# Graph network, four edge layers on one core: gathers held by their predecessor's descriptors instead of by writes on GpSimd, and fewer columns by TensorE

## The chip, the cores and the metric

One core of a Trainium2 chip runs the kernel. The metric is the device time of one execution in microseconds (us); lower is better. Of each kernel several executions are timed, and one more is recorded by the hardware profiler. The engines are called as in the profile: PE (TensorE), DVE (VectorE), ACT (ScalarE), POOL (GpSimd) and SP (SyncE, which issues transfers). POOLq is POOL's sequencer, the part that reads the instructions, holds waits and hands work to the engine.

## The reference

12,500 nodes have 32 features each; 400,000 edges, sorted by their destination, go from `src` to `dst`. Four layers follow one another, each with a layer norm, a ReLU, a message per edge and a sum over the edges of each node:

```
h = relu(layernorm(x));  x = x + segment_sum(h[src] * edge_attr_32, dst) / max(degree, 1) + h
h = relu(layernorm(x));  x = x + attention(h, h[src], dst; Wq, Wk, Wv, Wo)     # softmax over a node's edges
h = relu(layernorm(x));  x = x + segment_sum(h[src], dst) @ W
h = relu(layernorm(x));  x = x + segment_sum(tensor_product(h[src], edge_attr, W), dst)
```

What all four share is `h[src]`: 400,000 rows of 32 floats, picked by index out of a table of 12,500.

## The kernel before, in words

The edges are cut into 125 chunks of 3,200: 128 partitions by 25 columns (`J`) of 32 features. A layer is a loop of 25 turns (`TURNS`) of 5 chunks (`RING`), and `rows` has five buffers, one for each chunk of a turn. The rows `h[src]` of a chunk come to it in two ways, column by column; a column is 128 rows, one for each partition.

- **By POOL.** An indirect DMA (L492) takes 128 indices from `idx` and fetches 128 rows of `h_table` from HBM. POOL's cores write its descriptors, then the DMA engines move the rows.
- **By PE.** The table lies in SBUF too (`h_parts`). A column is a tile: 14 matmuls (L690) of a one-hot matrix with the table bring 14 candidates per edge into PSUM, and DVE picks the right one (L924 and L931, or L912 in layer 1). The one-hots are made by DVE in layer 0 (L887), stored to HBM (`hots`) and loaded again in layers 1 to 3; ACT converts them (L539, L546).

`PE_COLS[layer][chunk]` says how many of the 25 columns PE takes; POOL takes the rest. In sum over a turn that is 40, 32, 40 and 28 columns of 125 by PE in layers 0 to 3, that is 8, 6.4, 8 and 5.6 for a chunk.

POOL's program for a chunk waits until the buffer is free (`rows_used`) and the indices are there (`idx_loaded`), and then repeats for each column: a gather; a wait until the last write of `pace` has ended (`pause_ended`, L495), which together with an increment of `pause_begun` (L496) makes one record in the trace; and a write of zeros to `pace`, 128 x 288 floats (L497), which nobody reads. `pauses(l, t, r, j)` is the number of writes that have gone before, plus `START` (1), which the semaphore gets at the start.

DVE waits for a whole chunk's gathers and picked tiles before it turns the rows (L1028 in layer 0, L1163 in layer 1, L1293 in layer 2, `next_rows` in layer 3); it then frees the buffer. Up to five chunks may be ahead. What else a layer does for a chunk is DVE's scans and products, and on PE the attention's sums (L738, L745) or, in layer 3, the tensor product (`spread` L764, `couple` L773), between whose steps the next chunk's tiles stand.

Before and between the loops lie the node stages: layer norm, sums over a node's edges by 98 indirect DMAs (L509; in layer 1 also L471), and small matmuls.

Of the kernel before, what the change touches and what calls it, by code (L numbers as in the profile page):

```python
# [42 lines left out]
P = 128  # L43
# [12 lines left out]
FAR = -(2.0 ** 100)  # L56
H0 = 14

PE_COLS = ((8, 8, 8, 8, 8), (7, 7, 6, 6, 6), (8, 8, 8, 8, 8), (6, 6, 5, 5, 6))
PACE = 288  # L60
PE_MAX = max(max(c) for c in PE_COLS)
BIT_BUFS = (4, 4, 4, 4)
LOOK = (4, 4, 4, 4)
# [4 lines left out]
START = 1  # L68
# [9 lines left out]
def gnn_kernel(nc, x_in, src_c, src_pe, dst_c, dst_p, dst_blocks, pattern_c, sh_c, wq, wk, wv, wo, w2, w3,  # L78
# [10 lines left out]
    KEYS = PE_MAX * (NCH + 2)  # L89
    assert NCH % RING == 0 and KT % PT == 0 and all(sum(PE_COLS[l]) % b[l] == 0 for l in range(LAYERS) for b in (TILE_BUFS, BIT_BUFS))  # L90
    assert all(sum(PE_COLS[l]) % LOOK[l] == 0 and all(n <= m for n, m in zip(PE_COLS[l], PE_COLS[0])) for l in range(LAYERS))
    assert LOOK[0] == TILE_BUFS[0] and all(LOOK[l] == BIT_BUFS[l] for l in range(1, LAYERS))
# [18 lines left out]
    with ExitStack() as ctx:  # L111
        def sb(name, shape, dt=F32):
            return ctx.enter_context(nc.sbuf_tensor(name, shape, dt))

        def sem(name):
            return ctx.enter_context(nc.semaphore(name))

        def sems(name, n=RING):
            return [sem(f"{name}{r}") for r in range(n)]
# [10 lines left out]
        idx = sb("idx", [P, RING, J], I32)  # L130
# [33 lines left out]
        mz_parts = qh[:, 0:3 * P].rearrange("p (a m) -> p a m", m=P)  # L164
        h0_width = max(PE_COLS[1]) * P // 2
        h0_keys = [work[0:H0, k, at:at + h0_width].bitcast(I16) for k, at in ((1, 0), (2, 0), (13, CH - h0_width))]
        h0_hots = [work[:, k, at:at + h0_width].bitcast(BF16) for k, at in ((8, 0), (9, 0), (11, CH - h0_width))]
        far = work[:, 9, h0_width:h0_width + H0 * D // 2].bitcast(BF16)
        pace = sb("pace", [P, PACE])
        bit_hots.append(mz[:, CH - H1 * P // 2:CH].bitcast(BF16).rearrange("p (h n) -> p h n", n=P))  # L170
        bit_hots.append(nb[:, 0:H1 * P // 2].bitcast(BF16).rearrange("p (h n) -> p h n", n=P))
        spare = work[:, 13, 6 * PC - 3 * CH:CH]
# [63 lines left out]
        rows_gathered = [sems(f"rows_gathered{a}_") for a in range(2)]  # L236
# [25 lines left out]
        mix_in, mix_ps, mix_out = sem("mix_in"), sem("mix_ps"), sem("mix_out")  # L262
        x_ready, x_stored = sem("x_ready"), sem("x_stored")

        pause_begun, pause_ended = sem("pause_begun"), sem("pause_ended")

        block = ctx.enter_context(nc.Block())

        def use(l, t, more=0):

            return t + (l * TURNS + 1 + more)

        def gathers(l, t, r, more=0):

            each = 16 * (J - PE_COLS[l][r])
            return t * each + (each * (1 + more) + (16 * TURNS * (J - PE_COLS[l - 2][r]) if l >= 2 else 0))

# [1 line left out]

        per_turn = [sum(c) for c in PE_COLS]  # L280

        def pauses(l, t, r, j):

            before = sum(TURNS * (RING * J - per_turn[k]) for k in range(l))
            return t * (RING * J - per_turn[l]) + (before + sum(J - PE_COLS[l][k] for k in range(r)) + j + START)
# [172 lines left out]

        @block.gpsimd
        def _(pool):  # L460
            pool.sem_inc(pause_ended, START)
            for l in range(LAYERS):
                if l == 0:
                    pool.wait_ge(keep_made, 1)
                if l == 1:

                    pool.wait_ge(q_zeroed, 16 * TURNS)
                    for q in range(PIECES):
                        pool.wait_ge(q_ready, q + 1)
                        for k in range(q * PT, (q + 1) * PT):  # L470
                            nc.gpsimd.indirect_dma_start(  # L471
                                out=q_edges[:, :], out_offset=bass.IndirectOffsetOnAxis(ap=begin_row[:, k:k + 1], axis=0),
                                in_=node_rows[:, k * D:(k + 1) * D], in_offset=None).then_inc(q_scattered, 16)

                    pool.wait_ge(first_loaded, 16)
                    pool.wait_ge(q_stored, 16 * PIECES)
                    nc.gpsimd.indirect_dma_start(
                        out=first_q[:, :], out_offset=None, in_=q_table[:, :],
                        in_offset=bass.IndirectOffsetOnAxis(ap=first_idx[:, :], axis=0)).then_inc(first_gathered, 16)
                    pool.wait_ge(first_gathered, 16)  # L480
                    pool.wait_ge(q_scattered, 16 * KT)
                    pool.dma_start(q_chunks[0, 0:P:D, 0:D], first_q[:, :]).then_inc(first_stored, 16)
                for a in range(2):
                    pool.wait_ge(h_stored[a], 16 * ((PIECES * (l + 1) + 1 - a) // 2))
                pool.wait_ge(parts_ready, PIECES * (l + 1))
                with pool.Fori(0, TURNS) as t:
                    for r in range(RING):
                        pool.wait_ge(rows_used[r], use(l, t, START - 1))
                        pool.wait_ge(idx_loaded[r], use(l, t) * 16)
                        pool.sem_inc(chunk_begun, 1)  # L490
                        for j in range(J - PE_COLS[l][r]):
                            nc.gpsimd.indirect_dma_start(  # L492
                                out=rows[:, r, j * D:(j + 1) * D], out_offset=None, in_=h_table[:, :],
                                in_offset=bass.IndirectOffsetOnAxis(ap=idx[:, r, j:j + 1], axis=0)).then_inc(rows_gathered[l % 2][r], 16)
                            pool.wait_ge(pause_ended, pauses(l, t, r, j))  # L495
                            pool.sem_inc(pause_begun, 1)  # L496
                            nc.gpsimd.memset(pace[:, :], 0.0).then_inc(pause_ended, 1)  # L497
                if l == 0:
                    pool.wait_ge(block_ready, 1)
                    for k in range(KT):  # L500
                        nc.gpsimd.indirect_dma_start(  # L501
                            out=blocks[:, k, :], out_offset=None, in_=dst_blocks[:, :],
                            in_offset=bass.IndirectOffsetOnAxis(ap=end_row[:, k:k + 1], axis=0)).then_inc(block_gathered, 16)
                    pool.wait_ge(node_index_ready, 1)
                for r in range(RING):
                    pool.wait_ge(outs_stored[r], 16 * (l + 1) * TURNS + START)
                table, width = (attn, 2 * D) if l == 1 else (sums, D)
                for k in range(KT):
                    nc.gpsimd.indirect_dma_start(  # L509
                        out=node_rows[:, k * width:(k + 1) * width], out_offset=None, in_=table[:, :],  # L510
                        in_offset=bass.IndirectOffsetOnAxis(ap=end_row[:, k:k + 1], axis=0)).then_inc(node_gathered[k // PT], 16)
# [1027 lines left out]
```

## Time and profile before

| | |
|---|---|
| median of 3 runs | 16,096.28 us (16,094.55 to 16,126.25) |
| span of the profiled execution | 14,816.7 us |
| the profiled execution's own time | not given by the page |
| busy: PE, DVE, ACT, POOL | 12,890.3, 9,612.6, 3,874.6, 12,431.7 us |
| gathers by POOL (L492) | 9,000 |
| writes of `pace` (L497) | 9,000 |
| mean granted clock of PE | 0.948 |

The span reaches from the first to the last instruction in the trace. The busy time of POOL does not hold the gaps between its instructions. A gather's record ends when its descriptors are written, not when its rows have arrived. In the chain of waits "issue" is time in which an engine waited for nothing that the profile shows.

### The profile page before, as it was taken

How to read it: one execution, taken by the hardware profiler on the slowest of the kernel's cores; microseconds unless marked ns; L12 is line 12 of the kernel's file. 1: busy time of each engine (PE TensorE's matmuls, PEld its weight loads, DVE VectorE, ACT ScalarE, POOL GpSimd, SP SyncE). 2: the span in 40 equal slices, each digit the busy share in tenths (PEclk: the TensorE clock that was granted, in tenths of full speed). 3: DMA queues.
4: the chain of work that ended last, by engine and by line, in shares of the span. 5: the costliest groups of instructions: out<-in, count | busy, mean ns of one | idle time of the engine just before them, and what ended most of it. 6: DMA issues, size and time to landing. Idle time of an engine off the chain costs nothing.

```text
span 14816.7 us, 226154 instructions
## 1 busy us (share of the span) xinstructions
PE 12890.3 (87%) x57644; PEld 10677.8 (72%) x57644; DVE 9612.6 (65%) x13223; ACT 3874.6 (26%) x4265; POOL 12431.7 (84%) x18594
## 2 busy tenths in 40 slices
PE   7999999992699999999689999999769999999996
PEld 6888888881577777777578888888756666767764
DVE  7666666664577777777666666666656665666665
ACT  2222222220233333333222222222211111111111
POOL 6888888887888888888778888888888888888884
PEclk9999999995899999999889999999989999999998
DMA  5444444442344444444345555545433333333332
GB/s 174 148 148 157 157 155 151 149 151 46 101 123 122 124 124 123 122 123 124 90 119 130 129 130 128 131 127 131 110 76 87 86 90 83 90 86 87 87 86 56
DMA packets 1340717, 1727.48 MB, mean 117 GB/s; under 512 B 501932, under 2 KB 1145566, under 8 KB 1339646
## 3 DMA queue, kind: packets, MB, share of 16 engines
q10 hardware_dynamic: 705956, 1154.87, 24.6%
q1 hardware_dynamic: 327194, 407.86, 9.6%
q0 software_dynamic: 306880, 158.96, 7.6%
q14 instruction: 668, 5.47, 0.1%
q8 instruction: 19, 0.31, 0.0%
HBM read 1140.23 MB, written 580.36 MB: 116 GB/s over the span
## 4 chain that ended last, share of the span: by engine, by line
POOL 41%; issue 32%; PE 20%; DVE 5%; POOLq 1%; DMA 0%; DVEq 0%; ACT 0%; ACTq 0%; SPq 0%
POOL rows L492 22%; POOL pace L497 16%; PE psum L690 12%; PE psum L773 7%; POOL outs L509 2%; PE psum L764 2%; DVE work L1340 1%; DVE work L1315 1%; POOLq L496 1%; POOL q_edges L471 1%; POOL work L501 1%; DVE tile_rows L924 0%; DVE work L1323 0%; DVE rows L931 0%; DVE outs L1347 0%
## 5 line engine op out<-in xcount | busy, mean ns | idle before, releaser
L690 PE MATMUL psum<-h_parts,one_hot 128*128 128x448 f32 x49406 | 10813.2, 377 | 482.0 <-ACT one_hot L539 262.4
L690 PEld LDWEIGHTS psum<-h_parts,one_hot 128*128 128x128 f32 x49406 | 9428.8, 192 | 1500.6 <-ACT one_hot L539 313.0
L492 POOL DMA_INDIRECT rows<-h_table,idx x9000 | 8662.9, 963 | 1966.9 <-POOL pace L497 1537.1
L546 ACT ACTIVATE one_hot<-keys 128x896 fp32r<-128x896 bf16 x2533 | 2359.9, 950 | 6435.5 <-PE psum L690 4314.0
L497 POOL MEMSET pace<- 128x288 f32 x9000 | 3213.9, 357 | 18.1 <-issue 13.2
L924 DVE TENSOR_TENSOR tile_rows<-psum,h_mask 128x448 f32<-128x448 f32 x2722 | 1686.2, 619 | 1252.3 <-PE psum L690 991.3
L931 DVE TENSOR_REDUCE rows<-tile_rows 128x32 f32<-128x448 f32 x2722 | 1677.0, 616 | 58.9
L773 PE MATMUL psum<-work,bd_t 128*128 128x512 f32 (+1 forms) x3500 | 1359.2, 514 | 240.1 <-DVE work L1323 141.3
L1323 DVE TENSOR_TENSOR work<-psum,work 128x800 f32<-128x800 f32 x875 | 862.7, 988 | 920.9 <-PE psum L764 864.2
L773 PEld LDWEIGHTS psum<-work,bd_t 128*128 128x128 f32 x3500 | 654.9, 193 | 764.4 <-issue 443.4
L912 DVE TENSOR_REDUCE rows<-psum 128x32 f32<-128x448 f32 x807 | 503.1, 623 | 792.0 <-PE psum L690 741.7
L539 ACT ACTIVATE one_hot<-work 128x896 fp32r<-128x896 bf16 x506 | 482.0, 953 | 1493.3 <-DVE work L887 1493.3
L539 ACT ACTIVATE one_hot<-bit_hot 128x896 fp32r<-128x896 bf16 x506 | 482.6, 954 | 883.4 <-DVE bit_hot L887 880.5
L1028 DVE STREAM_TRANSPOSE psum<-rows 128x800 f32<-128x800 f32 x125 | 128.2, 1026 | 864.0 <-DMA rows<-h_table,idx 864.0
L686 PE MATMUL psum<-work 128*128 128x448 bf16 x807 | 296.3, 367 | 308.0 <-DVE work L904 223.6
L745 PE MATMUL psum<-work 128*128 128x512 f32 x1500 | 524.1, 499 | 0.0
L509 POOL DMA_INDIRECT outs<-sums,end_row x294 | 291.6, 992 | 258.3 <-DMA sums<-outs 147.0
L686 PEld LDWEIGHTS psum<-work 128*128 128x128 bf16 x807 | 78.2, 97 | 501.6 <-DVE work L904 276.3
L745 PEld LDWEIGHTS psum<-work 128*128 128x128 f32 x1500 | 284.2, 189 | 210.3 <-issue 179.8
L764 PE MATMUL psum<-work,sel 120*128 120x512 bf16 x1750 | 427.4, 337 | 0.0
L1163 DVE STREAM_TRANSPOSE work<-rows 128x800 f32<-128x800 f32 x125 | 213.7, 1710 | 207.7 <-DMA rows<-h_table,idx 188.4
L1293 DVE STREAM_TRANSPOSE psum<-rows 128x800 f32<-128x800 f32 x125 | 128.2, 1026 | 289.7 <-DMA rows<-h_table,idx 289.7
(202 smaller groups left out, 6198.1 us busy)
## 6 DMA issues: line engine op xcount, KB each, us to landing
keys<-hots ACTq DMA_DIRECT2D x2542, 224.0 KB
keep_in<-keep_flat SPq DMA_DIRECT2D x2000, 100.0 KB
sums<-outs ACTq DMA_DIRECT2D x375, 400.0 KB
rows<-h_table,idx POOLq DMA_INDIRECT x9000
hots<-bit_hot ACTq DMA_DIRECT2D x506, 224.0 KB
hots<-work ACTq DMA_DIRECT2D x506, 224.0 KB
attn<-outs ACTq DMA_DIRECT2D x125, 800.0 KB
edge_in<-pattern_c SPq DMA_DIRECT2D x125, 400.0 KB
```

Of the source, the lines that this page charges most:

```text
L492: nc.gpsimd.indirect_dma_start(out=rows[:, r, j * D:(j + 1) * D], out_offset=None, in_=h_table[:, :], in_offset=bass.IndirectOffsetOnAxis( ...
L497: nc.gpsimd.memset(pace[:, :], 0.0).then_inc(pause_ended, 1)
L509: nc.gpsimd.indirect_dma_start(out=node_rows[:, k * width:(k + 1) * width], out_offset=None, in_=table[:, :], in_offset=bass.IndirectOffse ...
L539: nc.scalar.activation(one_hots[i % LOOK[l]][:, :, :], bit_hots[i % BIT_BUFS[l]], ACT.Copy).then_inc(one_hot_cast, 1)
L546: nc.scalar.activation(one_hots[i % LOOK[l]][:, :, :], loaded_hots[i % BIT_BUFS[l]], ACT.Copy).then_inc(one_hot_cast, 1)
L690: last = nc.tensor.matmul(banks[TILE_BANKS[l][b]][:, 0:H0 * D], one_hots[hot][:, h1, :], h_parts[:, part, h1 * H0 * D:(h1 + 1) * H0 * D], ...
L745: last = nc.tensor.matmul(acc_wide[:, cols], mz_parts[:, part, :], rows_in[:, cols], start=(part == 0), stop=(part == 2))
L764: last = nc.tensor.matmul(bcast[n % 2][:, cols], sel[0:SH_ROWS, n, :], shT[r][:, cols], start=True, stop=True)
L773: last = nc.tensor.matmul(acc_wide[:, cols], bd_t[:, n, :], weighted[n % 4][:, cols], start=(n == 0), stop=(n == PRODUCTS - 1))
L924: nc.vector.tensor_tensor(tile_rows[:, :].rearrange("p (f h) -> p f h", f=D), banks[TILE_BANKS[l][b]][:, 0:H0 * D].rearrange("p (f h) -> p ...
L931: nc.vector.reduce_sum(rows[:, chunk % RING, j * D:(j + 1) * D], tile_rows[:, :].rearrange("p (f h) -> p f h", f=D), axis=AX_X).then_inc(p ...
L1323: nc.vector.tensor_tensor(weighted[n % 4], bcast[n % 2], hT, ALU.mult).then_inc(weighted_ready, 1)
```

## The change

The write of `pace` and its tile go. A new semaphore `gather_written` is given to the gather as its `engine_sem`: POOL adds 1 to it when it has written the gather's descriptors. Ahead of each gather stands a wait on `gather_written` for the number of gathers before it, again with an increment behind it. `written` is the former `pauses`. Besides, PE takes 32, 24, 32 and 20 columns of a turn in place of 40, 32, 40 and 28, and POOL the rest; loops, keys and one-hots follow `PE_COLS`.

```diff
-PE_COLS = ((8, 8, 8, 8, 8), (7, 7, 6, 6, 6), (8, 8, 8, 8, 8), (6, 6, 5, 5, 6))
-PACE = 288
+PE_COLS = ((7, 7, 6, 6, 6), (5, 5, 5, 5, 4), (7, 7, 6, 6, 6), (4, 4, 4, 4, 4))
...
-        pace = sb("pace", [P, PACE])
...
-        pause_begun, pause_ended = sem("pause_begun"), sem("pause_ended")
+        gather_begun, gather_written = sem("gather_begun"), sem("gather_written")
...
-        def pauses(l, t, r, j):
+        def written(l, t, r, j):
...
-            pool.sem_inc(pause_ended, START)
+            pool.sem_inc(gather_written, START)
...
                         for j in range(J - PE_COLS[l][r]):
+                            pool.wait_ge(gather_written, written(l, t, r, j))
+                            pool.sem_inc(gather_begun, 1)
                             nc.gpsimd.indirect_dma_start(
                                 out=rows[:, r, j * D:(j + 1) * D], out_offset=None, in_=h_table[:, :],
-                                in_offset=bass.IndirectOffsetOnAxis(ap=idx[:, r, j:j + 1], axis=0)).then_inc(rows_gathered[l % 2][r], 16)
-                            pool.wait_ge(pause_ended, pauses(l, t, r, j))
-                            pool.sem_inc(pause_begun, 1)
-                            nc.gpsimd.memset(pace[:, :], 0.0).then_inc(pause_ended, 1)
+                                in_offset=bass.IndirectOffsetOnAxis(ap=idx[:, r, j:j + 1], axis=0),
+                                engine_sem=gather_written).then_inc(rows_gathered[l % 2][r], 16)
```

POOL before, in the loop of layer 0, around the border between its second and third chunk. REGISTER_ALU works out the number that the next wait compares with; `rows_used2` and `idx_loaded2` belong to the third chunk. Semaphore instructions have no row of their own; what they wait for is printed with the next instruction.

```order
L497 MEMSET pace 128x288 [waits pause_ended]
L492 DMA rows<-h_table,idx 128x32
L495 REGISTER_ALU
L497 MEMSET pace 128x288 [waits pause_ended]
L492 DMA rows<-h_table,idx 128x32 [waits rows_used2,idx_loaded2]
L495 REGISTER_ALU
L497 MEMSET pace 128x288 [waits pause_ended]
L492 DMA rows<-h_table,idx 128x32
```

POOL now, in the loop of layer 0, around the border between its first and second chunk; the lines have moved up by two.

```order
L492 DMA rows<-h_table,idx 128x32 [waits gather_written]
L490 REGISTER_ALU
L492 DMA rows<-h_table,idx 128x32 [waits gather_written]
L490 REGISTER_ALU [waits rows_used1,idx_loaded1]
L492 DMA rows<-h_table,idx 128x32 [waits gather_written]
L490 REGISTER_ALU
L492 DMA rows<-h_table,idx 128x32 [waits gather_written]
```

The wait has moved from behind the gather, where the write had it, to the front of the gather.

PE before, at the end of layer 3's loop body, where the tensor product of a chunk (L773, L764) and the tiles of the next chunk (L690) take turns:

```order
L690 MATMUL psum<-h_parts,one_hot 128x448 [waits tile_used,one_hot_cast]
L690 MATMUL psum<-h_parts,one_hot 128x448 x13
L769 REGISTER_ALU
L773 MATMUL psum<-work,bd_t 128x512 [waits weighted_ready]
L773 MATMUL psum<-work,bd_t 128x288
L679 REGISTER_ALU
L690 MATMUL psum<-h_parts,one_hot 128x448 [waits tile_used,one_hot_cast]
L690 MATMUL psum<-h_parts,one_hot 128x448 x13
L769 REGISTER_ALU
L773 MATMUL psum<-work,bd_t 128x512 [waits weighted_ready]
L773 MATMUL psum<-work,bd_t 128x288
```

PE now, at the same place:

```order
L771 MATMUL psum<-work,bd_t 128x512 [waits weighted_ready]
L771 MATMUL psum<-work,bd_t 128x288
L762 MATMUL psum<-work,sel 128x512 [waits weighted_ready]
L762 MATMUL psum<-work,sel 128x288
L767 REGISTER_ALU
L771 MATMUL psum<-work,bd_t 128x512 [waits weighted_ready]
L771 MATMUL psum<-work,bd_t 128x288
L767 REGISTER_ALU
L771 MATMUL psum<-work,bd_t 128x512 [waits weighted_ready]
L771 MATMUL psum<-work,bd_t 128x288
```

Two of the six tiles of 14 matmuls of this chunk have gone, from behind the last steps of the tensor product; four are left.

## Rows read from the trace of the kernel before

**Rows 1.** The page: busy time and the chain that ended last.

```profile
PE 12890.3 (87%) x57644; PEld 10677.8 (72%) x57644; DVE 9612.6 (65%) x13223; ACT 3874.6 (26%) x4265; POOL 12431.7 (84%) x18594
...
POOL 41%; issue 32%; PE 20%; DVE 5%; POOLq 1%; DMA 0%; DVEq 0%; ACT 0%; ACTq 0%; SPq 0%
```

**Rows 2.** The four loops: length; busy of PE, PEld, DVE, ACT, POOL; clock; DMA.

```profile
85.00:3380.00 3295.00, 3021.77 (x14208) 2715.00 (x14205) 2271.61 (x3666) 961.64 (x1009) 2871.65 (x4248) 0.97 0.48 153
3783.00:7286.00 3503.00, 3176.48 (x13869) 2537.50 (x13870) 2463.61 (x2534) 1244.38 (x1436) 3030.21 (x4636) 0.97 0.44 122
7497.00:10697.00 3200.00, 2986.04 (x14066) 2690.39 (x14064) 2072.21 (x3386) 921.97 (x1006) 2769.04 (x4238) 0.97 0.51 130
10852.00:14556.00 3704.00, 3466.44 (x14587) 2566.43 (x14587) 2279.77 (x2689) 646.08 (x680) 3152.31 (x4837) 0.98 0.33 87
```

**Rows 3.** The page's line groups on POOL: busy, mean ns, idle before.

```profile
L492 POOL DMA_INDIRECT rows<-h_table,idx x9000 | 8662.9, 963 | 1966.9 <-POOL pace L497 1537.1
L497 POOL MEMSET pace<- 128x288 f32 x9000 | 3213.9, 357 | 18.1 <-issue 13.2
```

**Rows 4.** Timeline of POOL in layer 3: start, duration, idle before.

```profile
13200.25 0.95 POOL L492 DMA_INDIRECT rows<-h_table,idx  x1 [0.17 <-POOL pace L497]
13201.19 0.36 POOL L497 MEMSET pace<- 128x288 f32 x1
13201.72 0.95 POOL L492 DMA_INDIRECT rows<-h_table,idx  x1 [0.17 <-POOL pace L497]
...
13209.71 0.95 POOL L492 DMA_INDIRECT rows<-h_table,idx  x1 [5.22 <-issue]
```

**Rows 5.** Line groups in each loop: layer 0 (two rows), layers 1, 2, 3.

```profile
L690 PE MATMUL psum<-h_parts,one_hot 128*128 128x448 f32 x14112 | 3012.6, 375 | 262.5 <-ACT one_hot L539 262.4
L492 POOL DMA_INDIRECT rows<-h_table,idx x2120 | 2116.3, 998 | 419.9 <-POOL pace L497 360.6 <-issue 59.3
L492 POOL DMA_INDIRECT rows<-h_table,idx x2318 | 2205.0, 951 | 461.1 <-POOL pace L497 400.8 <-issue 60.2
L492 POOL DMA_INDIRECT rows<-h_table,idx x2118 | 2015.1, 951 | 420.9 <-POOL pace L497 363.4 <-issue 57.5
L492 POOL DMA_INDIRECT rows<-h_table,idx x2418 | 2299.5, 951 | 526.4 <-POOL pace L497 408.7 <-issue 117.7
```

**Rows 6.** Timeline of POOL after layer 3's loop: a gather without `pace`.

```profile
14700.93 0.94 POOL L509 DMA_INDIRECT outs<-sums,end_row  x1 [0.30 <-issue]
```

**Rows 7.** Chain of waits, a turn boundary of layer 1: start, us, what.

```profile
4193.10 0.02 POOLq L490
4193.12 0.53 issue
4193.64 0.04 POOLq L495
...
4193.86 0.95 POOL rows L492
```

**Rows 8.** Chain of waits, a turn boundary of layer 0.

```profile
870.58 0.02 POOLq L490
...
871.38 0.46 POOL rows L492
```

**Rows 9.** Chain of waits, within a turn of layer 0.

```profile
3000.75 0.37 POOL pace L497
...
3001.15 0.02 POOLq L496
```

**Rows 10.** Timeline of POOL, the last gather before the boundary of rows 7.

```profile
4189.99 0.95 POOL L492 DMA_INDIRECT rows<-h_table,idx  x1 [0.17 <-POOL pace L497]
```

**Rows 11.** Busy time between the loops of layers 0 and 1.

```profile
3380.00:3783.00 403.00, 44.29 (x153) 30.25 (x153) 120.72 (x229) 22.92 (x33) 290.24 (x303) 0.54 0.19 39
```

**Rows 12.** Chain of waits in layer 3: one tile.

```profile
13002.54 2.89 PE psum L690 x14
```

**Rows 13.** Waits in total: who waited for whom, us, times, longest.

```profile
DVE psum L1028 <- DMA rows<-h_table,idx: 864.0, 116, 10.2
```

## The prediction

> **What bounds the kernel now.** I read the page first, then the busy time of the four edge loops, then POOL's line groups, its timeline and the chain of waits, because the change is on POOL's queue.
>
> The page's busy shares [rows 1] say PE 87% and POOL 84%, which does not decide it. The chain that ended last gives POOL 41%, "issue" 32% and PE 20%; the reader should see that "issue" is larger than PE and ask whose it is. The stretches of the four loops [rows 2] last 3295, 3503, 3200 and 3704 us, in sum 13,702 of the span's 14,816.7; PE is busy 3022, 3176, 2986 and 3466 us in them, so it has 214 to 327 us to spare in each. POOL's rows [rows 3] hold 9,000 gathers and 9,000 writes of `pace`. In its timeline [rows 4] gathers start at 13200.25 and 13201.72, and so on: 0.95 us of gather, 0.36 of write, 0.17 until the next gather, 1.47 in all. 9,000 x 1.47 = 13,230 us, 97% of the loops' 13,702. So POOL's cadence, gaps included, is the bound in every layer, and the "issue" of the chain is mostly POOL's. The other 472 us are turn boundaries, single waits, and the longer gathers of layer 0 (998 ns against 951 in the others [rows 5]). Outside the loops lie 14,816.7 - 13,702 = 1,115 us.
>
> The page gives the span of the profiled execution and no time of its own for it. The median of the runs, 16,096.3, is 1,279.6 above the span. I first work out the new span, then treat these 1,280 us apart, since no row says where they are.
>
> **The change, part by part.**
>
> *Counts.* Per turn of five chunks the columns by TensorE fall from 40, 32, 40, 28 to 32, 24, 32, 20: 8 fewer in each layer. With 25 turns and four layers that is 800 tiles less on PE (and on ACT and DVE) and 800 gathers more on POOL: 9,800. SP's index loads stay; its key loads, and ACT's loads of hots, get fewer.
>
> *The write goes.* Each gather loses 0.36 us of write and the 0.17 behind it. What would be left if gathers simply followed one another is visible in layer 3's last gathers [rows 6]: 0.94 plus 0.30 of idle, 1.25 us. That is the lower bound of the new cadence.
>
> *The wait comes in front of the gather.* This is the term that decides. Before, the wait (record L496) stands between a gather and its own write, and it waits for the write before; the next gather has already been handed to the engine when it is held. The code order of the rows around the wait shows it: gather, wait, write, gather, wait. POOL's sequencer therefore prepares gather j+1 while gather j runs. After, the order is wait, gather, wait, gather, and each wait asks for the gather directly before it. Everything that the sequencer does for a gather now begins after its predecessor has ended.
>
> How long that takes is seen wherever the engine is empty and the sequencer begins late. At a turn boundary of layer 1 [rows 7] the wait L490 ends at 4193.12; the sequencer gets to the next instruction, L495, at 4193.64; the gather starts at 4193.86 and ends at 4194.81. So 0.74 us from the end of the wait to the start, of which some 0.53 are the sequencer's work on the gather. A boundary of layer 0 [rows 8] has 870.60 to 871.38, 0.78. The step from an engine's end to the end of the wait that it releases is in the chain at 3001 [rows 9]: the write ends at 3001.12, the wait's record at 3001.17, 0.05. New cadence: 0.95 + 0.05 + 0.74 to 0.78 = 1.74 to 1.78; I take 1.76. A completion signal that comes later than the end of the record would add to that: behind a gather the next one starts after 0.30 [rows 6] and behind a write after 0.17 [rows 4], so up to 0.13 may belong to the gather's own end. Upper bound 1.89.
>
> The Trainium skill, "DMA: Bandwidth & Descriptors", section on the anatomy of one DMA on the gpsimd path, puts the sequencer's dispatch of such a DMA at about 50 ns. By that figure the handover would be some 0.05 + 0.05 + 0.17, the cadence an estimated 1.22 us and the time an estimated 14,840 us. The boundary rows, 0.53 us in that place, say otherwise, and I go by them.
>
> *Loops.* 9,800 x 1.76 = 17,248 us. Of the 472 us around the cadence: at the boundary of layer 1 the last gather starts at 4189.99 [rows 10] and the next at 4193.86 [rows 7], 3.87 us, which branch and code take; over the cadence this is 2.40 before and 2.11 after, so about 96 boundaries give back 28. Layer 3 has 117.7 us of idle "issue" before its gathers against 57.5 to 60.2 elsewhere [rows 5]; the surplus are waits for a free buffer such as the 5.22 us at 13209.71 [rows 4], and they go when POOL is the late one: 58. Left: 386. Loops 17,634, span 17,634 + 1,115 = 18,749.
>
> *The tiles that leave PE.* Layer 0 has PE busy 3022 us for 14,112 matmuls, 1,008 tiles [rows 2, 5], 3.0 us each; 800 tiles take 2,400 us from PE. That is worth nothing here, because the cover is on the other side: per chunk of layer 0 PE needs 24.2 - 1.6 x 3.0 = 19.4 us and POOL 18.6 x 1.76 = 32.7. In layer 3, PE 27.7 - 4.8 = 22.9 and POOL 21 x 1.76 = 37.0. Nothing else comes near. One thing can turn against this: where PE has little to do its granted clock is low, 0.54 in the stretch between layers 0 and 1 [rows 11]. A tile takes 2.89 us [rows 12] at the full 2.4 GHz; were it always at the 1.2 GHz level, 6.4 tiles would need 37 us in a chunk of layers 0 and 2, 4.3 over POOL, 1,075 us in all. PE would then be busy all the time and not at that level, so I cost it at zero and keep it for the upper end.
>
> *Behind the new wait* stand only POOL's own gathers. Who waits for these is DVE: already 864 us for layer 0's rows [rows 13]. These waits grow; they are the same time seen from the other side and are not added.
>
> *The 1,280 us.* From both sides: if they lie outside the span, or on POOL, they stay (1,280; in proportion to the span 1,620); if in the timed executions PE was slower than in the profiled one, and with its 214 us of room became the bound, they vanish, as PE is now far from it (0). No row decides. I take 1,280, since the profile shows POOL and not PE as the bound: 18,749 + 1,280 = 20,029, say 20,030 us, 24% slower.
>
> **The rivals.**
>
> *The 1,280 us were PE's.* For it: PE is 92% busy in layer 0's loop, so a small loss of clock would make it the bound. Against it: granted clock is 0.97 to 0.98 in the loops. Time 18,750, still slower.
>
> *The wait costs no preparation: faster.* The gather itself could carry the wait in POOL's queue, so that it is already prepared when released, or the signal could come early enough to hide the step. Then the cadence is 1.25 [rows 6]. Loops 9,800 x 1.25 + 490 = 12,740, span 13,855, time 15,135, 6% faster; PE, at 22.9 us against POOL's 26.3 per chunk in layer 3, lets it happen. It decides for faster below a cadence of (13,702 - 450) / 9,800 = 1.352 us. For it: the order prints the wait with the gather. Against it: it prints L497's wait with the write in the same way, and in the trace that wait is a record of its own, POOLq L496, in front of the instruction [rows 9]. The Trainium skill, "Perfetto Trace Analysis", section on the SWDGE DMA instruction, has an instruction decoded and pushed into the wait queue before its semaphores are looked at. By that rule a wait carried by the gather would hide the 0.53 us and give this rival's time; the trace's separate record is what speaks against its use here.
>
> *Nothing changes.* A cadence of 1.352 within a few hundredths, by part of the preparation being hidden: time near 16,096. No row gives such a value; it is only what lies between 1.25 and 1.74.
>
> **How the numbers follow.** Forecast (cadence 1.76, the 1,280 stay) 0.61; the 1,280 were PE's 0.24; no preparation 0.13; nothing changes 0.02, half of it within 0.2%, the rest shared. 0.2% (32 us) is about what a measurement of this kernel can tell from no change. Faster 0.13, same 0.01, slower 0.86. The range holds the first two: from 18,750 less 450 for a handover shorter by 0.05 us, 18,300, up to 20,030 plus 980 for one longer by 0.10 us (short of the bound of 0.13), about 21,000.
>
> **What would show it.** Right: gathers of unchanged 0.95 us, an idle gap of 0.79 to 0.83 us before each, a start every 1.74 to 1.78 us in all four layers; PE under 65% busy with no gain from it; DVE's wait for gathered rows in thousands of us; about 9,800 gathers and a span near 18,750. Wrong: a gap of 0.3 us, which is the faster rival; gathers longer than 1 us, a contention I have not counted; time less span much under 1,000 us with the cadence right, the rival on the 1,280; or a PE clock near 0.5 inside the loops.

## The result and the profile after

The changed kernel took **18,327.8 us** (median of 3 runs, 18,314.0 to 18,333.0), the kernel before 16,096.3: a ratio of 1.1375 [1.1337, 1.1413], slower. The profiled execution is the one of 18,314.0 us, with a span of 18,311.2: 2.8 us lie outside the span. For the kernel before that difference had been 1,280 us. In every later execution on record, of whichever kernel, it is 2 to 5 us, so the profiled and the timed executions of the kernel before cannot have been alike. Further on, the kernel before took 14,815 us in two sets of runs, 15,291 and 16,258 in two others. Ratios are therefore taken within a set, and where a comparison crosses sets the text says so.

The page of the changed kernel: busy time, the clock in 40 slices, the chain that ended last [rows 1], and the groups of gathers and of the wait for them [rows 3, 13].

```profile
PE 11192.6 (61%) x46158; PEld 9111.6 (50%) x46158; DVE 8579.3 (47%) x11612; ACT 3113.7 (17%) x3459; POOL 9867.9 (54%) x10394
...
PEclk8777777775778888888777777787768888888887
...
issue 42%; DMA 37%; POOL 15%; POOLq 3%; DVE 2%; PE 0%; ACT 0%; another core or an unknown queue 0%; ACTq 0%; DVEq 0%; SPq 0%
...
L492 POOL DMA_INDIRECT rows<-h_table,idx x9800 | 9292.2, 948 | 8151.0 <-DMA rows<-h_table,idx 5398.7
...
L1026 DVE STREAM_TRANSPOSE psum<-rows 128x800 f32<-128x800 f32 x125 | 128.3, 1027 | 2077.6 <-DMA rows<-h_table,idx 2077.6
```

No engine is busy for two thirds of the span, and yet POOL sets the end: its idle time in front of gathers went from 1,967 to 8,151 us. It is put down to "DMA rows" and "issue"; the first is the landing of an earlier gather that happened to come last before the start, and nothing on POOL waits for landings. DVE's wait for layer 0's gathered rows went from 864 to 2,078 us.

The timeline of POOL after, in layer 0 (start, duration, idle before), answers to [rows 4]. It is typical: 9,533 of the 9,800 gathers start 0.76 to 0.80 us after their predecessor has ended.

```profile
3700.68 0.94 POOL L492 DMA_INDIRECT rows<-h_table,idx  x1 [0.78 <-issue]
3702.41 1.24 POOL L492 DMA_INDIRECT rows<-h_table,idx  x1 [0.78 <-issue]
...
3706.16 0.94 POOL L492 DMA_INDIRECT rows<-h_table,idx  x1 [0.78 <-issue]
3707.88 0.94 POOL L492 DMA_INDIRECT rows<-h_table,idx  x1 [0.78 <-issue]
```

And the chain of waits there, which takes the gap of 0.78 us apart, as [rows 7, 9] did for the kernel before:

```profile
3700.68 0.94 POOL rows L492
3701.62 0.03 issue
3701.66 0.02 POOLq L491
3701.67 0.52 issue
3702.19 0.03 POOLq L490
3702.22 0.18 issue
3702.41 1.24 POOL rows L492
```

The gather ends at 3701.62; the wait's record (L491) ends at 3701.67; the sequencer then works 0.52 us on the next gather, which starts 0.21 later: 0.05 + 0.73. A gather starts every 1.73 us (median 1.725), where it was 1.47.

The four loops after, against [rows 2]:

```profile
73.00:4187.00 4114.00, 2557.86 (x11413) 2330.41 (x11413) 1929.01 (x3066) 767.17 (x806) 2234.67 (x2325) 0.79 0.37 111
4592.00:9028.00 4436.00, 2784.02 (x10939) 2174.04 (x10939) 2315.54 (x2333) 1063.80 (x1244) 2385.64 (x2525) 0.80 0.32 87
9294.00:13371.00 4077.00, 2555.10 (x11297) 2327.16 (x11296) 1801.49 (x2986) 741.04 (x809) 2196.14 (x2325) 0.79 0.37 91
13542.00:18142.00 4600.00, 3187.54 (x12225) 2216.69 (x12224) 2073.73 (x2362) 476.86 (x502) 2475.15 (x2625) 0.82 0.24 62
```

In sum 17,227 us, against 13,702: 3,525 more, in every layer. PE is 62 to 69% busy, and its granted clock, which was 0.97 to 0.98 in these loops, is 0.79 to 0.82, without making it the bound.

### The profile page after: what moved, and what is told of

Its sections match the earlier page's. It is cut to its first block, busy times and chain, and to the rows that moved or that the text cites. A ratio compares the mean times of both kernels' runs of the same rounds, so it can differ in the third digit from the quotient of the medians.

```text
span 18311.2 us, 186561 instructions
## 1 busy us (share of the span) xinstructions
PE 11192.6 (61%) x46158; PEld 9111.6 (50%) x46158; DVE 8579.3 (47%) x11612; ACT 3113.7 (17%) x3459; POOL 9867.9 (54%) x10394
## 4 chain that ended last, share of the span: by engine, by line
issue 42%; DMA 37%; POOL 15%; POOLq 3%; DVE 2%; PE 0%; ACT 0%; another core or an unknown queue 0%; ACTq 0%; DVEq 0%; SPq 0%
DMA rows<-h_table,idx 37%; POOL rows L492 14%; POOLq L490 2%; POOLq L491 1%; POOL outs L507 1%; POOL q_edges L469 1%; DVE work L1108 0%; DVE work L1110 0%; PE psum L688 0%; POOLq L488 0%; DVE h_parts L849 0%; DVE work L842 0%; DVE work L1106 0%; DVE ln L832 0%; DVE work L835 0%
## 5 line engine op out<-in xcount | busy, mean ns | idle before, releaser
L492 POOL DMA_INDIRECT rows<-h_table,idx x9800 | 9292.2, 948 | 8151.0 <-DMA rows<-h_table,idx 5398.7
L688 PE MATMUL psum<-h_parts,one_hot 128*128 128x448 f32 x38122 | 8837.0, 394 | 3073.5 <-ACT one_hot L537 1506.9
L688 PEld LDWEIGHTS psum<-h_parts,one_hot 128*128 128x128 f32 x38122 | 7819.5, 207 | 3853.0 <-issue 1652.4
L544 ACT ACTIVATE one_hot<-keys 128x896 fp32r<-128x896 bf16 x1928 | 1790.0, 949 | 8230.6 <-issue 3931.3
L771 PE MATMUL psum<-work,bd_t 128*128 128x512 f32 (+1 forms) x3500 | 1497.6, 560 | 1418.5 <-DVE work L1338 1394.0
L922 DVE TENSOR_TENSOR tile_rows<-psum,h_mask 128x448 f32<-128x448 f32 x2118 | 1310.1, 619 | 665.4 <-PE psum L688 317.0
L929 DVE TENSOR_REDUCE rows<-tile_rows 128x32 f32<-128x448 f32 x2118 | 1305.3, 616 | 44.9
L1313 DVE STREAM_TRANSPOSE work<-rows 128x800 f32<-128x800 f32 x124 | 206.7, 1667 | 1305.0 <-DMA rows<-h_table,idx 1305.0
L910 DVE TENSOR_REDUCE rows<-psum 128x32 f32<-128x448 f32 x605 | 377.9, 625 | 872.0 <-PE psum L688 579.0
L1161 DVE STREAM_TRANSPOSE work<-rows 128x800 f32<-128x800 f32 x125 | 208.7, 1670 | 1155.5 <-DMA rows<-h_table,idx 1144.0
L620 ACT ACTIVATE work<-keep_in 128x800 f32<-128x800 f32 x125 | 108.8, 871 | 1848.2 <-issue 1847.9
```

Of the source, the lines that this page charges most:

```text
L492: nc.gpsimd.indirect_dma_start(out=rows[:, r, j * D:(j + 1) * D], out_offset=None, in_=h_table[:, :], in_offset=bass.IndirectOffsetOnAxis( ...
L544: nc.scalar.activation(one_hots[i % LOOK[l]][:, :, :], loaded_hots[i % BIT_BUFS[l]], ACT.Copy).then_inc(one_hot_cast, 1)
L688: last = nc.tensor.matmul(banks[TILE_BANKS[l][b]][:, 0:H0 * D], one_hots[hot][:, h1, :], h_parts[:, part, h1 * H0 * D:(h1 + 1) * H0 * D], ...
L771: last = nc.tensor.matmul(acc_wide[:, cols], bd_t[:, n, :], weighted[n % 4][:, cols], start=(n == 0), stop=(n == PRODUCTS - 1))
L910: nc.vector.reduce_max(rows[:, chunk % RING, j * D:(j + 1) * D], banks[TILE_BANKS[l][b]][:, 0:H0 * D].rearrange("p (f h) -> p f h", f=D), ...
L922: nc.vector.tensor_tensor(tile_rows[:, :].rearrange("p (f h) -> p f h", f=D), banks[TILE_BANKS[l][b]][:, 0:H0 * D].rearrange("p (f h) -> p ...
```

## The experiments

Each was timed beside the kernel before on the same chip. The kernel before is named with its time in that set.

**The kernel before once more, unchanged.**

> The kernel before, unchanged, for a trace whose own time is known. The first trace had a span of 14,817 us, 1,280 below the runs' 16,096; the changed kernel's span is only 3 us below its time. Theory P (PE was the bound in the timed executions): time 16,096, span within 20 us of it, gathers still every 1.47 us within a chunk, but POOL waits for free buffers (over 1,000 us of idle more than in the first trace), tiles of PE slower than 2.89 us, mean granted clock below 0.9. Theory Q (the 1,280 us are POOL's): gathers every 1.6 us, clock near 0.95. Theory F (fixed, outside the span): span 14,820, time 16,096.

14,815.9 us, against 14,815.1 for its twin in the same set (1.0001 [0.9992, 1.0011]); span 14,815.0. All three theories missed, as each had expected 16,096: here the timed executions are like the profiled one. The 1,280 us were no fixed time outside the span.

**The wait alone**, with the columns of before.

```diff
-PE_COLS = ((7, 7, 6, 6, 6), (5, 5, 5, 5, 4), (7, 7, 6, 6, 6), (4, 4, 4, 4, 4))
+PE_COLS = ((8, 8, 8, 8, 8), (7, 7, 6, 6, 6), (8, 8, 8, 8, 8), (6, 6, 5, 5, 6))
```

> The new wait alone, with the columns of before (9,000 gathers). Theory H (the handover sets the cadence, 1.73 us for each gather, and POOL is the bound): 9,000 x 1.73 = 15,570 plus the 1,360 us that the changed kernel's span has beside its gathers: 16,930 us. Rival P (PE at the old columns is the bound at about 16,096 for either cadence): between 16,930 and 17,500, as both engines are then close to their limits. Rival C (the shift of columns, not the wait, made it slower): about 16,100.

16,871.4 us, 1.1392 [1.1373, 1.1411] of 14,815.1. Theory H had 16,930. The wait, put in the place of the write, costs 2,056 us by itself; rival C is out, and the range of rival P begins above the time.

**The columns alone**, with the writes of `pace`.

```diff
-PE_COLS = ((8, 8, 8, 8, 8), (7, 7, 6, 6, 6), (8, 8, 8, 8, 8), (6, 6, 5, 5, 6))
+PE_COLS = ((7, 7, 6, 6, 6), (5, 5, 5, 5, 4), (7, 7, 6, 6, 6), (4, 4, 4, 4, 4))
```

> The new columns alone, with the writes of pace kept (9,800 gathers every 1.47 us). Theory P (PE bound the timed executions of before): POOL becomes the bound, 9,800 x 1.47 + 1,400 = 15,800 us, faster than before. Theory Q (POOL's cadence is 1.61 in timed executions): 9,800 x 1.61 + 1,400 = 17,180 us. Theory F (a fixed 1,280 outside): 17,080 us.

15,800.9 us, 1.0668 [1.0650, 1.0686]: 986 us slower than before. The sum 9,800 x 1.47 + 1,400 = 15,800 held, but with POOL as the bound of both kernels, not with PE as that of before. Of the 1,176 us that 800 gathers more cost, 800 tiles less on PE can have given back 190 at most.

**One gather of slack.** A gather waits for the one before its predecessor.

```diff
-            pool.sem_inc(gather_written, START)
+            pool.sem_inc(gather_written, START + 1)
```

> The changed kernel with one gather of slack: a gather waits for the one before its predecessor (the semaphore starts one higher). Theory H: the sequencer prepares a gather while the last one runs, the gap falls from 0.78 to 0.30 us, a gather starts every 1.25 us: 9,800 x 1.25 + 1,400 = 13,650 us, unless PE or DVE becomes the bound, then up to 14,800. Rival (the wait itself, not its being just ahead, costs 0.78 us): 18,330 us.

13,475.5 us, 0.9099 [0.9084, 0.9114] of 14,815.1, with the same count of instructions as the changed kernel. The timeline of POOL:

```profile
3000.81 0.94 POOL L492 DMA_INDIRECT rows<-h_table,idx  x1 [0.31 <-DMA rows<-h_table,idx]
3002.06 0.94 POOL L492 DMA_INDIRECT rows<-h_table,idx  x1 [0.30 <-DMA rows<-h_table,idx]
```

The gap is 0.30 us, a gather starts every 1.25: the value of [rows 6]. It is not the wait that costs, but that it asks for the gather just ahead. The changed kernel itself was not timed in this set. By the run with the wait alone and 800 gathers more at 1.725 us, an estimate, it would take 18,251 us here; it took 18,328 in the first measurement. From that to 13,475 are 4,852 us, across two sets, or 0.495 for each of the 9,800 gathers; the gap's 0.48 gives 4,700 of them.

The second set of runs was another matter: here the kernel before took 16,257.8 us.

**The changed kernel once more.**

> The changed kernel, unchanged, beside runs of the kernel before that take 14,815 us. If POOL's cadence of 1.73 us sets its time wherever it runs, it takes 18,310 to 18,330 us here too, a ratio of 1.236, with the same line groups. If what made the first executions of before 1,280 us longer slowed the changed kernel as well, it takes about 17,000 us here.

18,318.2 us, 1.1276 [1.1235, 1.1318] of 16,257.8. The expected time held. The ratio of 1.236 did not, since it was the kernel before that took another time than expected. What lengthens the kernel before is hardly seen in the changed kernel's time, which is within 0.4% of the 18,251 estimated for a set at 14,815. It is seen in its traces. The waits of PE's tiles for "issue" (us, times, longest), first in the trace of the result, then in this one:

```profile
PE psum L688 <- issue: 895.8, 72, 15.8
PE psum L688 <- issue: 1032.1, 81, 16.4
```

In the set where the kernel before took 14,815 us no kernel's tiles have such a wait among their causes. In these two traces they are few and long, 12 us on average, and stand at the start of tiles; POOL's cadence hides them.

**Neither wait nor write.**

```diff
-            pool.sem_inc(gather_written, START)
...
-                            pool.wait_ge(gather_written, written(l, t, r, j))
-                            pool.sem_inc(gather_begun, 1)
...
-                                in_offset=bass.IndirectOffsetOnAxis(ap=idx[:, r, j:j + 1], axis=0),
-                                engine_sem=gather_written).then_inc(rows_gathered[l % 2][r], 16)
+                                in_offset=bass.IndirectOffsetOnAxis(ap=idx[:, r, j:j + 1], axis=0)).then_inc(rows_gathered[l % 2][r], 16)
```

> The new columns with neither the wait nor the write: gathers follow one another freely. Theory H: nothing but the exposed handover costs, one gather of slack already hides all of it, so the cadence is 1.25 us as with the slack, 13,470 us. Rival G (queued gathers without any wait disturb each other, which would be a reason for pacing them): gathers longer than 0.95 us or transfers that hold up POOL, over 14,000 us.

20,353.9 us, 1.2529 [1.2483, 1.2575] of 16,257.8. Theory H missed by 6,900 us. Rival G was right that something is disturbed, but not in its place: gathers still take 948 ns on average and within a chunk start every 1.25 us. The timeline of PE, where one tile's matmuls follow one another with no wait between them:

```profile
2966.92 0.53 PE L684 MATMUL psum<-h_parts,one_hot 128*128 128x448 f32 x1 [0.87 <-issue]
2968.32 0.53 PE L684 MATMUL psum<-h_parts,one_hot 128*128 128x448 f32 x1 [0.87 <-issue]
...
2970.41 1.44 PE L684 MATMUL psum<-h_parts,one_hot 128*128 128x448 f32 x2 [0.87 <-issue]
2972.54 39.73 PE L684 MATMUL psum<-h_parts,one_hot 128*128 128x448 f32 x186 [0.69 <-issue]
```

And that of POOL at the same time:

```profile
2947.00 0.94 POOL L489 DMA_INDIRECT rows<-h_table,idx  x1 [12.03 <-DMA idx<-src_c]
...
2967.34 0.94 POOL L489 DMA_INDIRECT rows<-h_table,idx  x1 [0.30 <-issue]
2968.59 0.94 POOL L489 DMA_INDIRECT rows<-h_table,idx  x1 [0.30 <-issue]
3008.45 0.94 POOL L489 DMA_INDIRECT rows<-h_table,idx  x1 [38.92 <-DMA idx<-src_c]
```

The busy time of the stretch in three pieces (columns as in [rows 2]):

```profile
2949.80:2958.40 8.60, 8.60 (x44) 7.72 (x42) 4.87 (x10) 2.80 (x3) 6.65 (x7) 1.00 0.58 189
2958.40:2969.60 11.20, 5.38 (x12) 3.00 (x11) 0.00 (x0) 0.05 (x1) 8.50 (x9) 0.60 0.16 34
2972.50:3008.40 35.90, 35.86 (x168) 33.41 (x168) 33.29 (x53) 13.15 (x14) 0.00 (x0) 0.93 0.36 126
```

POOL starts a run of gathers at 2947.00. PE goes on at full rate for 11 us, then does 12 matmuls in 11.2 us, singly or in pairs, while DVE does nothing, ACT almost nothing and the DMA engines are 16% busy. POOL's last gather ends at 2969.5, and from 2972.5 on PE runs 186 matmuls without a gap. The program has its waits before a tile and none within it.

The rest of the trace repeats this. Starts of two matmuls of one tile, with no wait between them, lie over 1 us apart 1,570 times in this execution. In all traces of kernels whose gathers start every 1.47 or 1.73 us there is one such case, and none in the two of the kernel with slack and the new columns. POOL's gathers come in 436 runs; in 196 of them such cases occur, and in most of these the first comes 12 to 18 us after the run's first gather.

So PE starts its instructions late, and it does so while POOL's gathers follow closely. That PE lacks instructions is a reading of this and not shown, and what would hold them up is open. Their loading by DMA does not explain it: in the loop of layer 0, from 400 to 4500 us, the trace has no packet on the queues that load instructions, and in the whole execution it has fewer than that of the kernel before, 38 and 16 against 668 and 19 (packets, MB, share):

```profile
q14 instruction: 38, 0.31, 0.0%
q8 instruction: 16, 0.26, 0.0%
```

Before these matmuls PE waits for "issue" 3,262 us in all, and unlike the changed kernel in many short pieces:

```profile
PE psum L684 <- issue: 3262.3, 2420, 31.9
```

POOL then waits in its turn, 38.92 us here and 6,072 in sum, for index loads that SP issues late. SP issues this one at 3004.20, behind a load of keys (L393) that had waited 53.7 us for DVE's one-hots, and DVE had stood still with PE.

**Slack with the old and with balanced columns.**

Both start the semaphore one higher, as above, and differ from each other in the columns: first the old ones, then the balanced ones.

```diff
+PE_COLS = ((8, 8, 8, 8, 8), (7, 7, 6, 6, 6), (8, 8, 8, 8, 8), (6, 6, 5, 5, 6))
```

```diff
+PE_COLS = ((8, 7, 7, 7, 7), (6, 6, 6, 5, 5), (8, 7, 7, 7, 7), (5, 5, 5, 5, 4))
```

> The wait with one gather of slack, and the columns of before: 9,000 gathers. If POOL stays the bound: 13,475 - 800 x 1.256 = 12,470 us. But PE is busy 3,030, 3,178, 2,982 and 3,464 us in the four loops with these columns, against 2,669, 2,920, 2,669 and 3,046 us that POOL would need. So theory B (PE becomes the bound): loops of 3,060 to 3,560 us, in sum 13,000, time 14,100, slower than with the new columns.

> The wait with one gather of slack, and columns that balance POOL (1.256 us a gather) against PE (3.0 to 3.2 us a tile beside its other work): 36, 28, 36 and 24 of a turn, 9,400 gathers. POOL needs 22.4, 24.4, 22.4 and 25.4 us for a chunk, PE 21.7, 22.8, 21.5 and 25.2. Theory B: POOL just remains the bound, 13,475 - 400 x 1.256 = 12,970 us; where the two engines do not fit together so closely, up to 13,400.

21,872.1 us (1.3470 [1.3420, 1.3520]) and 21,152.6 (1.3019 [1.2971, 1.3067]), beside 16,257.8. Both expectations missed by 7,700 and more. The group of the first says why the balance was beside the point:

```profile
L688 PE MATMUL psum<-h_parts,one_hot 128*128 128x448 f32 x49406 | 12135.0, 400 | 3812.9 <-issue 2869.1 <-DVE tile_rows L922 918.9 <-ACT one_hot L544 19.0
```

2,869 us of "issue" before PE's tiles again, in 2,305 pieces, and 2,978 us in the second. Matmuls of one tile start over 1 us apart 1,475 and 1,500 times; some in the first:

```profile
699.93 0.53 PE L688 MATMUL psum<-h_parts,one_hot 128*128 128x448 f32 x1 [2.28 <-issue]
702.77 0.53 PE L688 MATMUL psum<-h_parts,one_hot 128*128 128x448 f32 x1 [2.31 <-issue]
704.87 0.53 PE L688 MATMUL psum<-h_parts,one_hot 128*128 128x448 f32 x1 [1.57 <-issue]
```

With these columns and in this set a wait with slack does not protect.

**A third set: before and slack again.** Here the kernel before took 14,819.0 us.

> The kernel before, unchanged, once more: in the first set of runs it took 14,815 us, in the second 16,258, and no trace is there of an execution of the longer kind. Theory S (the engines' instruction supply is what the longer executions lack, and gathers that follow each other closely are what takes it): if this set is of the longer kind, the trace shows the cadence of 1.47 us within chunks unchanged, and over 1,000 us more of idle issue in front of PE's tiles (L690) than the 0 of the short kind; time 16,100 to 16,300. Theory P (a slower clock of PE): tiles longer than 2.89 us, no such gaps. If the set is of the short kind: 14,815.

14,817.1 us; the short kind once more, so neither S nor P was tested.

> The changed kernel with one gather of slack, once more. It took 13,475 us in the first set. Theory S: in a set of the longer kind it loses the most, since its gathers come every 1.25 us: 19,000 to 21,000 us, as no_wait did with 20,354. If only the kernel without any wait suffers and the slack of one protects: 13,475 in either kind.

13,473.9 us, 0.9093 [0.9078, 0.9108]. It repeats the first set. Its time beside an execution of before that takes 16,000 is not known. A longer write of `pace` (440 elements) was to go with these two and did not fit into SBUF.

**A fourth set: balanced columns and before.** Here the kernel before took 15,290.9 us.

> One gather of slack and the balanced columns (36, 28, 36, 24), once more. It took 21,153 us in the set where before took 16,258. Theory B with S: in a set where before takes 14,815 POOL or PE is the bound and nothing is short of supply: 12,970 us, up to 13,400 where the two do not fit together. In a set of the longer kind it repeats 21,150.

20,918.1 us, 1.3688 [1.3649, 1.3727]. That is 1% below the 21,150 expected for a set of the longer kind, although the kernel before is only 476 us longer here than at 14,815. PE waits 2,832 us for "issue" before its tiles, in 2,384 pieces.

> The kernel before, unchanged. Where its runs take 14,815 us the trace is as the first one. Where they take 16,100 to 16,300, theory S: cadence 1.47 us within chunks, over 1,000 us of idle issue in front of PE's tiles; theory P: tiles longer than 2.89 us and no such gaps.

15,292.8 us, on the chip that gave 14,815 in the first set. So the chip alone does not decide it. Its groups of tiles and of gathers, to be held against [rows 3]:

```profile
L690 PE MATMUL psum<-h_parts,one_hot 128*128 128x448 f32 x49406 | 11019.8, 381 | 540.8 <-issue 246.7 <-ACT one_hot L546 197.0 <-ACT one_hot L539 89.9
...
L492 POOL DMA_INDIRECT rows<-h_table,idx x9000 | 8662.5, 963 | 2262.9 <-issue 1213.1 <-POOL pace L497 618.3 <-DMA idx<-src_c 431.5
```

The chain that ended last, against [rows 1], and a tile of this execution:

```profile
PE 48%; issue 21%; DVE 13%; POOL 13%; another core or an unknown queue 3%; ACT 1%; ACTq 1%; DVEq 0%; POOLq 0%; DMA 0%; SPq 0%
...
12002.69 2.88 PE psum L690 x14
```

In the short kind POOL had 41% of the chain and PE 20%; here PE has 48% and POOL 13%. POOL is ahead and PE behind. POOL ends the gathers of layer 1 at 7350.77, and DVE begins to turn the layer's last chunk 102 us later; in the short kind (the third set's trace) it does so 1.5 us after the last gather:

```profile
7349.82 0.95 POOL L492 DMA_INDIRECT rows<-h_table,idx  x1 [0.17 <-issue]
7453.14 1.71 DVE L1163 STREAM_TRANSPOSE work<-rows 128x800 f32<-128x800 f32 x1 [0.22 <-DVEq L916]
...
7276.80 0.95 POOL L492 DMA_INDIRECT rows<-h_table,idx  x1 [0.17 <-POOL pace L497]
7279.28 1.68 DVE L1163 STREAM_TRANSPOSE work<-rows 128x800 f32<-128x800 f32 x1 [1.47 <-DMA rows<-h_table,idx]
```

So theory P is half right: PE leads the chain in this execution. The sign that it named for POOL, over 1,000 us more of waits for free buffers, did not come. POOL's idle time in front of gathers rose by 296 us only, all of it as waits for index loads (134 to 432); those put down to "issue" and to `pace` are 1,831 us together, as before (1,832). The slower clock is hardly there either: this tile takes 2.88 us as in [rows 12], and the mean clock is 0.933, not below 0.9; that of the executions of 16,258 us is 0.922 to 0.924 on record. Yet PE's busy time grew by 222 us, from 12,890 to 13,112, and a part of that may be the clock's. Theory S has a weak sign, 247 us of "issue" before PE's tiles where the short kind has none among its causes, and not the 1,000 that it asked for. Matmuls of one tile start over 0.6 us apart 76 times, against once or twice in the short kind's traces, which is next to nothing in time. This execution is only 492 us longer than the short kind by its span, not the 1,281 and 1,443 us of the others. An execution of 16,100 us was never traced.

## Why the prediction was right, point by point

**POOL's cadence was the bound: right for the trace that was read.** Where the kernel before takes 14,815 us, 800 tiles taken from PE with the cadence kept made it slower by 986 us, 84% of the 1,176 us that 800 gathers more cost. For the executions of 16,096 us, with which the changed kernel was compared, it is not shown, and in the one longer execution that was traced PE leads the chain.

**The wait exposes the sequencer's work: right, shown.** The step had 0.05 us to the end of the wait and 0.74 to 0.78 to the start; measured were 0.05 and 0.73. The cadence is 1.725 and not 1.76 us, 343 us over all gathers. The gap of 0.78 us lies just below the 0.79 to 0.83 that I had named as the sign. Slack of one takes the whole price away, so it is not the wait as such. The boundary rows' 0.53 us came out as 0.52. The Trainium skill, "DMA: Bandwidth & Descriptors", section on the anatomy of one DMA on the gpsimd path, gives about 50 ns for the sequencer's dispatch. For this indirect gather the trace does not agree, and the measurement decides.

**The signal's delay: right to leave it out.** Of the bound of 0.13 us more, 0.10 went into the range; the chain has 0.03 us from the gather's end to the wait's record.

**The rest of the loops: right within 70 us.** 17,227 - 9,800 x 1.725 = 322 us, forecast 386. Outside the loops 1,084, forecast 1,115. Together with the cadence this gives the span: 18,311 against 18,749.

**The tiles that left gave nothing, and the clock cost nothing: right.** PE is 61% busy; the clock fell more than I had thought (0.79) and hid in the slack.

**The 1,280 us: the step that failed.** I let them stay, because the profile shows POOL as the bound and a fixed or POOL-sided time would stay. Measured: 2.8 us in their place. This term alone carries 1,277 of the 1,702 us between the forecast of 20,030 and the result. The error behind it was to read the kernel before's median and its trace as the same kind of execution. The rival that set the term to zero had 18,750, the nearest number, and a mechanism that fits the traces better: PE was the bound in the timed executions, and the time vanished when PE was relieved. The longer execution that was traced speaks for it, with PE 48% and POOL 13% of the chain, though it was not one of 16,096 us. Its reason, a PE slowed by its clock, is borne out in small part at most (0.933 against 0.948); why PE falls behind stays open.

**The range: luck in part.** The time fell into it 28 us above its lower end, and only since the range was drawn to hold the rival too. That lower end was also added up loosely: 0.05 us over 9,800 gathers are 490 us and not 450, which would give 18,260. The sum of the faster rival takes 490 us around the cadence where the forecast takes 386, without a reason.

**The faster rival, a gather that carries its own wait, did not come.** In the trace the wait is a record of POOLq in front of the gather (L491), as argued. A gather that does carry the wait was not tried. Its cadence of 1.25 was right for the kernel with slack.

**What stays open.** What makes the kernel before take 14,815 us in one set and 15,291, 16,096 or 16,258 in another is open, and so is whether the same thing decides for the kernels with closely spaced gathers. Those took 13,475 us in the two sets with before at 14,815 (new columns and slack), and 20,354 to 21,872 in the two others (no wait, or slack with more columns). No kernel with a cadence of 1.25 ran in both kinds of set; that the set and not the kernel's other differences decides is likely from the kernel with neither wait nor write, which differs from the one with slack only in the wait and its two semaphores, but it is not shown. That instructions are what is missing is read from PE's gaps within tiles and was not varied by itself.

## What to carry to other kernels

In this kernel a wait for the direct predecessor on the same engine puts the sequencer's preparation of the next instruction on the path; ask for the one before it, and the preparation hides. That was faster in the two sets at 14,815 us only; its relatives in the two other sets were far slower, so such a change is to be timed in more than one set. Read such a preparation from a place in the trace where the engine is empty and the sequencer comes late, such as a loop's turn: one such row gave 0.74 us, which with 0.05 for the end of the wait is the gap of 0.78 us within 0.01. And compare a profile's span with the timed runs before building on their difference; where they disagree by more than some microseconds, take neither as the base without a run that has both.

## What the runs showed of the hardware that was not expected

Where gathers start every 1.25 us on POOL, PE can start its instructions late: matmuls of one tile, 0.2 us apart when all is well, came 1.4 us apart (and 2.1 to 2.8 us in the kernel with the old columns), with the DMA engines 16% busy. PE held out for some 11 us from the first gather. In two other sets gathers every 1.25 us did nothing of the kind. At 1.73 us between gathers nothing of this is seen in the time: the changed kernel took 18,328 and 18,318 us beside 16,096 and 16,258, and the one with the old columns kept to its sum beside 14,815. A kernel's cost was thus not its own: the same program took 14,815, 15,291, 16,096 and 16,258 us, each within 0.8% inside its set, and the version that was fastest in one set has relatives that were the slowest in another. The chain of waits went with it: POOL leads it in the traces of the short kind, PE in the longer one.
